# Second attention of a two-layer transformer kernel: queries computed with tokens over partitions, turned by DMA, and its side stages and first units placed anew

## The chip, the cores and the metric

The kernel runs on one core of one Trainium2 chip, in one launch. The metric is the device time of that launch in microseconds, as a median over runs.

## The reference, cut to what matters

2048 tokens (32 batches of 64) of width 512 pass four blocks, each added to x after a layer norm: a first cross attention, a feed-forward with 4-bit weights, a second cross attention, and a small routed memory with a gate. The change lies in the second attention:

```python
q = (layernorm(x) @ q_proj_w.T).reshape(B, Q, 32, 128)      # 32 query heads, 8 key heads
k = (ctx @ k_proj_w.T)...;  v = (ctx @ v_proj_w.T)...
q = w_q * q * rsqrt(mean(q * q, -1) + eps)                  # rmsnorm over the head's 128
k = w_k * k * rsqrt(mean(k * k, -1) + eps)
attn = softmax(q @ k.T / sqrt(128) + attention_mask)
x = x + (attn @ v) @ o_proj_w.T
```

The first attention has rotary positions in place of the norms.

## The kernel before, in words

**Units.** Both attentions are cut into 32 units: a group g of 8 (4 query heads, one key head) times a chunk c of 4 (512 tokens, 8 batches). `UNITS` lists them in order. Between the attentions lies the feed-forward, 24 steps of (s, c). Every product is made of halves: each operand is held as a 16-bit high part and a 16-bit low part, and three matmuls (`THREE`) replace one.

**Five engines, five programs.** `sync`, `tensor`, `scalar`, `vector` and `gpsimd` are written out by hand in program order and joined by semaphores (`signal`s). A wait holds up all that is behind it on that engine. SP (`sync`) has the only queue of DMAs: it issues the loads of weights, and the DMA transposes.

**A unit on TensorE** (`units`, L1160): `scores(u)`, then `front(u + 1)`, which is keys and values of unit u+1 (`keys_values`, L801) and four query tiles (`queries`, L817); then four tiles of the output product of unit u-1 (`output`, L865), and `weigh(u)` (L907), probabilities times values. In the second attention, `norm_q(u + 1)` (L886) stands between output tiles 2 and 3. PSUM has eight banks: the queries lie in 0, 1, 6, 7; keys and values in 2, 3; the scores in 4, 5; output tiles 0 to 3 in 2, 3, 0, 2; weighing in 0, 1, 6, 7. `bank(i, ...)` waits until what lay in the bank has been read.

**Queries of the second attention.** A head's query product has the head's 128 dimensions over partitions and 512 tokens along the row, the layout that scores needs. The norm is a sum over partitions, so ScalarE writes a high half (L1449), the squares (L1452) and the squares' high half (L1453); VectorE writes the query's low half (L2023); GpSimd writes the squares' low half (L2750); and TensorE sums the squares over partitions with 32 matmuls against a column of ones (L886). VectorE scales these sums (L2031), GpSimd raises them to the power -1/2 (L2758), and the softmax multiplies the scores by the result (L2082), then adds the mask (L2088).

**Keys of the second attention** have tokens over partitions. ScalarE sums their squares (L1423), VectorE multiplies by both norm weights (L2008), GpSimd takes the power (L2741) and scales (L2744). From unit 2 on ScalarE and GpSimd make the halves (L1430, L2735) and a DMA transpose turns them (L637); in units 0 and 1 TensorE turns them (`turn_k`, L874).

**Probabilities** are normalised on GpSimd (L2722), halved (L1470, L2729), and turned by DMA (L630), or by TensorE (L851, with L1477 and L2118 behind it) in units 0 and 31.

**Side stages.** `SIDE` is a table of other work, put by `plan(L, u, slot, stage)` at slots 0 to 9 of a unit: 0 after keys and values, 1 to 4 behind the query tiles, 5 to 8 behind the output tiles, 9 behind weighing. It holds the preparation of the next weights ("amax" L1330, "peak" L923, "scale" L1366, "low" L1933), layer norms ("ln_norm" L1499, "ln_turn" L936 and L1511, "ln_low" L1952), and the last block's stages. Weights of groups 0 and 1 of the second attention have their low halves made by GpSimd (L2686).

## Time and profile before

| | |
|---|---|
| median of 3 runs | 2425.37 us (2425.29 to 2427.68) |
| the profiled execution's own time | 2425.11 us |
| its span | 2423.3 us |
| granted TensorE clock, mean | 0.994 of 2.4 GHz |
| matmuls (PE) / weight loads | 2367.6 us, 98% / 1295.6 us, 53% |
| VectorE (DVE) / ScalarE (ACT) / GpSimd (POOL) | 67% / 52% / 51% |

The span is what the profiler records from the first to the last instruction; the time is some 2 us longer. PE stands for TensorE's matmuls, PEld for its weight loads, SPq for the queue of DMAs. "L886" is line 886 of the kernel. A row of the timeline merges neighbouring instructions of one line: start, duration, engine, line, operation, output<-inputs, shapes, count, and in brackets the idle time before with what ended it. A matmul's modelled end lies past its successor's start, so its cost on the path is the distance between starts.

### The profile page before, as it was taken

To read this page: it belongs to the slowest core of one execution; us is meant where nothing else is said; L and a number is where in the kernel's file an instruction comes from. 1 tells how busy PE (TensorE), PEld (TensorE's weight loads), DVE (VectorE), ACT (ScalarE), POOL (GpSimd) and SP (SyncE) were. 2 spreads that over 40 slices of the span, in tenths; PEclk is the share of its full clock that TensorE was granted. 3 is DMA by queue.
4 is the path that set the end of the run, shared out by engine and by line. 5 is a ranking of instruction groups with operands and counts; after the bars stand their busy time and mean duration, and the time that the engine had idled before them with its cause. 6 is when DMAs were issued, how large, how long until landed. Compare 5 with 4: busy or idle time off the path is not lost.

```text
span 2423.3 us, 45113 instructions
## 1 busy us (share of the span) xinstructions
PE 2367.6 (98%) x17668; PEld 1295.6 (53%) x17668; DVE 1625.1 (67%) x3133; ACT 1254.1 (52%) x2423; POOL 1227.8 (51%) x983
## 2 busy tenths in 40 slices
PE   8899999999999999999999999999999999999998
PEld 4455555555555555444444655555555555555554
DVE  7977777777777798754444666667666666656566
ACT  7666555656555545433232554555555555544443
POOL 4656566666666666233232445445555555445531
PEclk9999999999999999999999999999999999999999
DMA  6111121212121111011101011122121212221101
GB/s 211 45 45 36 44 53 27 53 27 53 32 53 31 42 40 28 27 44 36 44 11 29 27 31 28 44 53 62 36 62 36 62 36 62 53 43 27 27 14 70
DMA packets 216753, 108.13 MB, mean 45 GB/s; under 512 B 169280, under 2 KB 192480, under 8 KB 216544
## 3 DMA queue, kind: packets, MB, share of 16 engines
q1 hardware_dynamic: 216544, 105.25, 17.5%
q8 instruction: 142, 2.33, 0.4%
q14 instruction: 67, 0.55, 0.1%
HBM read 61.62 MB, written 4.19 MB: 27 GB/s over the span
## 4 chain that ended last, share of the span: by engine, by line
PE 65%; POOL 13%; DVE 11%; issue 5%; ACT 5%; DMA 0%; POOLq 0%; DVEq 0%; SPq 0%; ACTq 0%
PE PB L865 18%; PE PB L817 16%; PE PB L977 9%; PE PB L801 6%; PE PB L994 5%; POOL AR L2711 5%; POOL AR L2716 3%; POOL PSP L2729 2%; PE PB L907 2%; PE PB L842 2%; DVE AR L2128 2%; DVE WB L1933 2%; PE PB L773 2%; POOL AR L2706 1%; ACT JUNK L1330 1%
## 5 line engine op out<-in xcount | busy, mean ns | idle before, releaser
L865 PE MATMUL PB<-WB,AR 128*128 128x512 f16 x3072 | 685.5, 380 | 3.4 <-DVE XTB L1952 1.6
L817 PE MATMUL PB<-XTB,WB 128*128 128x512 f16 x3072 | 679.5, 380 | 1.2 <-DVE XTB L1952 0.7
L865 PEld LDWEIGHTS PB<-WB,AR 128*128 128x128 f16 x3072 | 298.3, 98 | 359.0 <-issue 11.1
L817 PEld LDWEIGHTS PB<-XTB,WB 128*128 128x128 f16 x3072 | 297.5, 98 | 345.3 <-issue 5.6
L2722 POOL TENSOR_TENSOR AR<-AR,SML 128x512 f32<-128x512 f32 x128 | 144.6, 1150 | 318.1 <-DVE SML L2113 318.1
L2143 DVE SCALAR_TENSOR_TENSOR X<-PB,SML,X 128x512 f32<-128x512 f32 x256 | 189.5, 747 | 169.4 <-PE PB L865 163.4
L1490 ACT ACTIVATE AR<-PB 128x512 f16<-128x512 f32 x256 | 132.0, 602 | 248.2 <-PE PB L907 248.2
L2023 DVE TENSOR_TENSOR AR<-PB,AR 128x512 f16<-128x512 f32 x128 | 88.2, 690 | 167.9 <-ACT AR L1453 167.9
L2711 POOL TENSOR_TENSOR AR<-AR,CST 128x512 f32<-128x512 f32 x128 | 183.0, 1430 | 33.9 <-ACT AR L1400 33.9
L977 PE MATMUL PB<-XTB,AR 128*128 128x512 f16 (+1 forms) x864 | 192.5, 379 | 0.0
L1994 DVE TENSOR_TENSOR AR<-AR 128x512 f16<-128x512 f32 x128 | 132.9, 1038 | 74.7 <-ACT AR L1406 74.5
L2716 POOL TENSOR_TENSOR AR<-AR 128x512 f32<-128x512 f32 x128 | 174.6, 1364 | 12.1 <-DVE AR L1985 2.3
L801 PE MATMUL PB<-WB,CTB 128*128 128x256 f16 x1536 | 173.1, 273 | 1.1 <-DVE WB L1933 0.9
L2128 DVE TENSOR_TENSOR AR<-PB,AR 128x512 f16<-128x512 f32 x256 | 158.6, 682 | 11.7 <-ACT AR L1490 11.7
L1985 DVE TENSOR_TENSOR AR<-PB,CST 128x512 f32<-128x512 f32 x128 | 88.2, 689 | 112.8 <-ACT AR L1400 112.8
L2758 POOL TENSOR_TENSOR SML<-SML 128x16 f32<-128x16 f32 (+1 forms) x33 | 98.4, 2982 | 128.9 <-DVE SML L2031 128.9
L1406 ACT ACTIVATE AR<-AR 128x512 f16<-128x512 f32 x128 | 80.5, 630 | 158.8 <-POOL AR L2716 157.4
L801 PEld LDWEIGHTS PB<-WB,CTB 128*128 128x128 f16 x1536 | 148.0, 98 | 18.7 <-issue 1.0
L2750 POOL TENSOR_TENSOR AR<-AR 128x512 bf16<-128x512 f32 x128 | 147.8, 1163 | 16.3 <-ACT AR L1453 16.3
L2702 POOL TENSOR_TENSOR AR<-AR,CST 128x512 f32<-128x512 f32 x32 | 44.6, 1394 | 216.7 <-ACT AR L1379 216.7
L2729 POOL TENSOR_TENSOR PSP<-AR,PSP 128x512 f16<-128x512 f32 x120 | 149.9, 1259 | 0.0
L2777 POOL TENSOR_TENSOR AR<-AR 128x512 f16<-128x512 f32 (+1 forms) x44 | 50.9, 1156 | 180.2 <-ACT AR L1574 180.2
(273 smaller groups left out, 3776.9 us busy)
## 6 DMA issues: line engine op xcount, KB each, us to landing
STG<-in_wo SPq DMA_DIRECT2D x14, 1024.0 KB
STG<-in_wq SPq DMA_DIRECT2D x13, 1024.0 KB
STG<-in_qw_gu SPq DMA_DIRECT2D x40, 128.0 KB
STG<-in_ctxT SPq DMA_DIRECT2D x4, 1024.0 KB
X<-in_x SPq DMA_DIRECT2D x4, 1024.0 KB, 10.3
out_x<-X SPq DMA_DIRECT2D x16, 256.0 KB, 2.4
STG<-in_wk SPq DMA_DIRECT2D x14, 256.0 KB
STG<-in_wv SPq DMA_DIRECT2D x14, 256.0 KB
```

Of the source, the lines that this page charges most:

```text
L801: m = pe.do.matmul(b[:, t2 * 256:(t2 + 1) * 256], CT[x][c][:, k, tok], wkv[y][:, k, :], start=n == 0, stop=n == 11)
L817: m = pe.do.matmul(b[:, :], wq[x][:, k, h * 128:(h + 1) * 128], XT[y][c][:, k, :], start=n == 0, stop=n == 11)
L865: m = pe.do.matmul(b[:, :], AT[x][:, h, t * 128:(t + 1) * 128], wo[y][:, h, :], start=n == 0, stop=n == 11)
L977: m = pe.do.matmul(b[0:wd, :], GUW[pl][x][:, k, cols], XT[y][c][:, k, :], start=e == 0, stop=e == 11)
L1994: dve.do.tensor_tensor(head_of(QT[1], h), by_batch(M1[h]), head_of(QT[0], h), ALU.subtract).then_inc(q_lo.of((0, u, h)), 1)
L2128: dve.do.tensor_tensor(lo, b[:, :].rearrange("p (b h q) -> p b h q", b=2, h=4), hi, ALU.subtract).then_inc(at_lo.of((L, u, j, odd)), 1)
L2143: dve.do.scalar_tensor_tensor(xs, PB[WB_OUT[t]][:, :], co(L, u, 0), xs, ALU.mult, ALU.add).then_inc(x_add.of((L, u, t)), 1)
L2711: pool.do.tensor_tensor(rt, rt, SINT.unsqueeze(1).to_broadcast([128, BC, SQ]), ALU.mult).then_inc(q_sin.of((u, h)), 1)
L2716: pool.do.tensor_tensor(M1[h], M1[h], RT[h], ALU.add).then_inc(q_add.of((u, h)), 1)
L2722: pool.do.tensor_tensor(v, v, RCT[:, cols].unsqueeze(2).to_broadcast([128, BC, SQ]), ALU.mult).then_inc(p_n.of((L, u, pair)), 1)
L2729: pool.do.tensor_tensor(PL[:, pair, :], SS[:, pair, :], PH[:, pair, :], ALU.subtract).then_inc(pl.of((L, u, pair)), 1)
L2750: pool.do.tensor_tensor(head_of(SQL, h), by_batch(M1[h]), head_of(SQH, h), ALU.subtract).then_inc(sql.of((u, h)), 1)
```

## The change

In the second attention:

- A query product is now one token tile of 128 by the group's four heads (512 columns): `XT` is stationary, the weights move. Two batches share a token tile, and `XT` of that norm is written with the tokens in the order query, then parity of the batch.
- ScalarE squares each head out of PSUM with a sum along the row (16 instructions of 128 columns), scales the four sums; GpSimd takes the power of 4 columns for each tile; ScalarE writes the scaled high halves (16 of 128 columns), VectorE the scaled low halves (16). SP turns them with three DMA transposes (2048, 1024 and 1024 columns). Scores read them with a step of two columns.
- The keys' scaling goes into their halves (4 instructions on ScalarE, 4 on VectorE); the product on GpSimd goes, and all units' keys are turned by DMA. `norm_q` and `turn_k` are gone from TensorE, `L2082` from the softmax, `L2744`, `L2735` and `L2750` from GpSimd.
- Layer norms and tail set-up use other banks and slots; weights' halves made by GpSimd in unit 1 move to slots 5 to 7.
- First units: keys and values of unit 1 and its first query tile precede unit 0's scores; unit 2's keys and values stand around unit 0's weighing; unit 0's probabilities are turned after query tile 2. In the first attention, the prologue's order and the slots of a layer norm and of chunk 2's preparation change.

```diff
+        QHP = [words(a, 1024, F16) for a in (10752, 5632)]
+        QHL = [QHP[t // 2][:, 1024 * (t % 2):1024 * (t % 2) + 1024] for t in range(4)]
+        QT_tiles = words(0, 2048, F16).rearrange("p (a n) -> p a n", n=128)
+        QT_rows = words(0, 2048, F16).rearrange("p (t a m o) -> p t a m o", t=4, a=4, o=2)
+        def rows_of(L, n, pair, b):
+            if L == 0:
+                return QT[n][:, (pair * BC + b) * 128:(pair * BC + b + 1) * 128]
+            return QT_rows[:, b // 2, 2 * n + pair, :, b % 2]
...
+            for half, (norm, turn, low) in enumerate(((0, 3, 3), (4, 6, 6)) if L == 0 else ((0, 2, 2), (3, 5, 6))):
...
-        plan(1, 1, 0, "scale", w(1, 1, 2))
+        plan(1, 1, 5, "scale", w(1, 1, 2))
-            plan(1, 1, 1 + half, "low", w(1, 1, 2), half)
+            plan(1, 1, 6 + half, "low", w(1, 1, 2), half)
-        plan_ln(1, 2, 2, 2)
-        plan_ln(1, 4, 2, 3)
+        for u, c in ((2, 2), (4, 3)):
+            plan(1, u - 1, 9, "ln_stats", 2, c)
+            for slot, *stage in ((4, "ln_norm", 0), (6, "ln_turn", 0), (6, "ln_low", 0), (6, "ln_norm", 1), (8, "ln_turn", 1),
+                                 (8, "ln_low", 1)):
+                plan(1, u, slot, stage[0], 2, c, *stage[1:])
...
+            def turn_q(u, part):                                   # SP
+                first, last = ((0, 2), (2, 3), (3, 4))[part]
+                for t in range(first, last):
+                    sp.wait_ge(q_hi, (1, u, t))
+                    sp.wait_ge(q_lo, (1, u, t))
+                if u > 0:
+                    sp.wait_ge(s_mm, (1, u - 1, 1))
+                else:
+                    sp.wait_ge(y_mm, (4, NC - 1, 3))
+                sp.do.dma_start_transpose(out=QT_tiles[:, 8 * first:8 * last, :],
+                                          in_=QHP[0] if part == 0 else QHL[first]).then_inc(qt_in.of((u, part), 16), 16)
...
+                    elif u < NU - 1:
+                        if by_dma(1, u):
+                            turn_p_pair(1, u, 0)
+                        turn_k(u + 1)
+                        if by_dma(1, u):
+                            turn_p_pair(1, u, 1)
+                        for part in range(3):
+                            turn_q(u + 1, part)
...
+            def queries_1(u, t):                                   # TensorE
+                b = bank(QB[t], (q_hi, (1, u, t)), (q_lo, (1, u, t)))
...
+                for k in range(KT):
+                    for x, y in THREE:
+                        m = pe.do.matmul(b[:, :], XT[x][c][:, k, t * 128:(t + 1) * 128], wq[y][:, k, :],
+                                         start=n == 0, stop=n == 11)
...
-            def turn_k(u):
-            def norm_q(u):
...
                 for u in range(NU - 1):                            # TensorE, units
                     scores(L, u)
                     front(L, u + 1, u)
...
+                    if (L, u) == (1, 0):
+                        keys_values(2, 0)
                     weigh(L, u)
                     side(L, u, 9)
+                    if (L, u) == (1, 0):
+                        keys_values(2, 1)
...
+            def squares_1(u, t):                                   # ScalarE
+                for h in range(4):
+                    n = 4 * t + h
+                    act.do.activation(M1[t][:, 128 * h:128 * h + 128], PB[QB[t]][:, 128 * h:128 * h + 128], ACTF.Square,
+                                      accum_out=RSQ[:, n:n + 1]).then_inc(q_sq.of((u, t)), 1)
+                act.wait_ge(q_sq, (u, t))
+                rs = RSQ[:, 4 * t:4 * t + 4]
+                act.do.activation(rs, rs, ACTF.Identity, scale=1.0 / DH, bias=eco(1, g, 0)).then_inc(q_ms.of((u, t)), 1)
+            def queries_1(u, t):
+                act.wait_ge(q_pow, (u, t))
...
+                for h in range(4):
+                    n = 4 * t + h
+                    act.do.activation(QHL[t][:, 128 * h:128 * h + 128], PB[QB[t]][:, 128 * h:128 * h + 128], copy,
+                                      scale=RSQ[:, n:n + 1]).then_inc(q_hi.of((1, u, t)), 1)
...
+                    for t in range(4):                             # ScalarE, front
+                        if (u, t) != (1, 0):
+                            squares_1(u, t)
+                        if t == 0 and by_dma(1, beside):
+                            halved_p(1, beside)
+                        if t == 1:
+                            halved_k(u)
+                        if t > 0:
+                            queries_1(u, t - 1)
+                        if (beside, t) == (0, 2):
+                            turned_p(1, 0)
+                        if t == 3:
+                            queries_1(u, 3)
+                        side(1, beside, 1 + t)
...
+            def low_1(u, t):                                       # VectorE
+                dve.wait_ge(q_pow, (u, t))
+                dve.wait_ge(q_hi, (1, u, t))
+                for h in range(4):
+                    n, cols = 4 * t + h, slice(128 * h, 128 * h + 128)
+                    dve.do.scalar_tensor_tensor(QHL[t][:, 512 + 128 * h:640 + 128 * h], PB[QB[t]][:, cols], RSQ[:, n:n + 1],
+                                                QHL[t][:, cols], ALU.mult, ALU.subtract).then_inc(q_lo.of((1, u, t)), 1)
...
+                    halved_k(u)                                    # VectorE, front
+                    for t in range(4):
+                        side(1, beside, 1 + t)
+                        low_1(u, t)
...
-                    for h in range(4):                             # GpSimd, front
-                        queries_1(u, h)
+                    for t in range(4):
+                        power_1(u, t)
+                        if t < 2 and by_dma(1, beside):
+                            halved_p(1, beside, t)
```

## Rows read from the trace of the kernel before

**Rows 1.** The page's first part: busy us, share of the span, instructions.

```profile
PE 2367.6 (98%) x17668; PEld 1295.6 (53%) x17668; DVE 1625.1 (67%) x3133; ACT 1254.1 (52%) x2423; POOL 1227.8 (51%) x983
```

**Rows 2.** Table of stretches: length; PE, PEld, DVE, ACT, POOL busy; clock; DMA share, GB/s.

```profile
1420.00:2340.00 920.00, 910.04 (x7543) 529.88 (x7541) 585.06 (x1215) 474.27 (x1084) 465.18 (x378) 0.99 0.20 44
```

**Rows 3.** TensorE's timeline of one typical unit of the second attention.

```profile
1908.00 2.75 PE L817 MATMUL PB<-XTB,WB 128*128 128x512 f16 x12
1910.59 7.93 PE L865 MATMUL PB<-WB,AR 128*128 128x512 f16 x36
1918.36 0.94 PE L886 MATMUL PB<-ONEB,AR 128*128 128x1 bf16 x32
1919.17 2.75 PE L865 MATMUL PB<-WB,AR 128*128 128x512 f16 x12
1921.85 1.48 PE L907 MATMUL PB<-AR 64*128 64x256 f16 x24
1923.27 1.57 PE L842 MATMUL PB<-AR 128*128 128x64 f16 x48
```

**Rows 4.** TensorE's timeline of the second attention's unit 0.

```profile
1382.96 0.60 PE L874 MATMUL PB<-CST,AR 128*128 128x128 f32 x4
1383.39 2.78 PE L801 MATMUL PB<-WB,CTB 128*128 128x256 f16 x24
...
1401.77 0.63 PE L874 MATMUL PB<-CST,AR 128*128 128x128 f32 x4 [1.55 <-ACT AR L1477]
...
1403.27 2.74 PE L907 MATMUL PB<-AR 64*128 64x256 f16 x24
```

**Rows 5.** TensorE in unit 1, and its waits at L886: total, times, longest.

```profile
1435.91 4.90 PE L865 MATMUL PB<-WB,AR 128*128 128x512 f16 x12
...
PE PB L886 <- POOL AR L2750: 4.6, 3, 4.0
```

**Rows 6.** TensorE's timeline of the first attention's start.

```profile
49.36 0.86 PE L842 MATMUL PB<-AR 128*128 128x64 f16 x24 [3.40 <-DVE AR L1994]
50.69 4.44 PE L817 MATMUL PB<-XTB,WB 128*128 128x512 f16 x12 [0.47 <-DVE WB L1933]
...
68.81 2.74 PE L907 MATMUL PB<-AR 64*128 64x256 f16 x24 [4.06 <-DVE AR L2118]
```

**Rows 7.** Weight loads by form: count, busy us, mean ns, idle before.

```profile
L886 PEld LDWEIGHTS PB<-ONEB,AR 128*128 128x128 bf16 x1024 | 30.1, 96 | 12.5 <-issue 6.2
L936 PEld LDWEIGHTS PB<-CST,LNB 128*128 128x128 f32 x192 | 21.4, 140 | 13.3 <-issue 8.2 <-DVE XTB L1952 2.2 <-DVE AR L2011 0.6
...
L923 PEld LDWEIGHTS PB<-IDB,SML 128*128 128x128 bf16 x55 | 5.4, 98 | 12.6 <-issue 4.3 <-DVE SML L1882 2.4 <-ACT JUNK L1330 0.4
```

**Rows 8.** ScalarE's timeline in the unit of rows 3.

```profile
1902.43 0.27 ACT L1423 ACTIVATE AR<-PB 128x128 f32<-128x128 f32 x1
1902.58 0.20 ACT L1423 ACTIVATION_READ_ACCUMULATOR AR<-PB 128x1 f32 x1
...
1907.01 1.17 ACT L1470 ACTIVATE PSP<-AR 128x512 f16<-128x512 f32 x2
...
1912.24 1.71 ACT L1366 ACTIVATE WB<-STG,SML 128x256 f16<-128x256 f32 x4
```

**Rows 9.** VectorE and GpSimd by form, 1700 to 2280 us: busy us, mean ns.

```profile
L2023 DVE TENSOR_TENSOR AR<-PB,AR 128x512 f16<-128x512 f32 x75 | 51.8, 691 | 95.4 <-ACT AR L1453 95.4
...
L2750 POOL TENSOR_TENSOR AR<-AR 128x512 bf16<-128x512 f32 x76 | 87.2, 1157 | 2.9 <-ACT AR L1453 2.9
...
L2741 POOL TENSOR_TENSOR SML<-SML 128x4 f32<-128x4 f32 x18 | 18.3, 1016 | 0.0
```

**Rows 10.** SP's transposes (ns min/median/max; landing), and a stretch that holds three.

```profile
L630 SPq DMA_TRANSPOSE AR<-PSP x120: 1232/1233/1442, 96.0 to 2324.3; - x120
...
DMA to landing us min/median/max: 3.0/3.1/5.0
...
1911.20:1917.00 5.80, 5.80 (x28) 2.65 (x27) 2.89 (x8) 2.75 (x7) 4.54 (x5) 1.00 0.69 130
```

More of the change, by code:

```diff
@@ L378, in plan_ln @@
                 plan(L, u - 1, 9, "ln_stats", i, c)
-            for half, (norm, turn, low) in enumerate(((0, 2, 2), (3, 5, 6))):
+            for half, (norm, turn, low) in enumerate(((0, 3, 3), (4, 6, 6)) if L == 0 else ((0, 2, 2), (3, 5, 6))):
                 plan(L, u, norm, "ln_norm", i, c, half)
@@ L529, in ln_banks @@
                 return 2, 3
-            return (4, 5) if (i, c) in IN_FFN else ((2, 3), (1, 6))[half]
+            if i == 2 and c > 1:
+                return (4, 3) if half else (4, 5)
+            return 4, 5
         def unpack_banks(s, k):
@@ L868, in output @@
                 m.then_inc(wo_mm.of((L, u, t)), 1)
-            def turn_k(u):
-                b = bank(4, (kt_hi, (1, u)), (kt_lo, (1, u)))
-                pe.wait_ge(k_mul, u)
-                for t in range(4):
-                    m = pe.do.transpose(b[:, t * 128:(t + 1) * 128], KF[:, t * 128:(t + 1) * 128], IDN)
-                m.then_inc(kt_mm.of(u), 1)
-            def norm_q(u):
-                bk = bank(5, (q_ms, u))
-                pe.wait_ge(q_sq, (u, 3))
-                pe.wait_ge(sql, (u, 3))
-                pe.wait_ge(ones_ok, "ones")
-                for pair in range(2):
-                    for b in range(BC):
-                        o = bk[:, pair * BC + b:pair * BC + b + 1]
-                        for n, s in enumerate((SQH, SQL)):
-                            m = pe.do.matmul(o, rows_of(s, pair, b), ONEB[:, 0:1], start=n == 0, stop=n == 1)
-                m.then_inc(qn_mm.of(u), 1)
             def weigh(L, u):
@@ L1281, in tensor @@
             keep_warm(8, 0)
[L1282 to L1283 removed]
+            queries_0(0, 0)
+            queries_0(0, 1)
+            queries_0(0, 2)
+            queries_0(0, 3)
             peak(w(0, 1, 0), 5)
[L1285 to L1286 removed]
             keys(1)
@@ L1303, in tensor @@
             keys_values(0, 0)
+            down(*FFN[-1])
             keys_values(0, 1)
-            down(*FFN[-1])
+            for t in range(4):
+                queries_1(0, t)
             ln_turn(2, 1, 1)
-            for h in range(4):
-                queries(1, 0, h)
             keys_values(1, 0)
-            turn_k(0)
             keys_values(1, 1)
-            norm_q(0)
+            queries_1(1, 0)
             units(1)
@@ L1856, in scalar @@
                 side("f", s, c, 3)
+            act.do.activation(TBL, CST[:, 0:1], ACTF.Exp).then_inc(t_act.of("table"), 1)
             values_1(0, 0)
             values_1(0, 1)
+            for t in range(4):
+                squares_1(0, t)
+                if t == 1:
+                    halved_k(0)
+                if t > 0:
+                    queries_1(0, t - 1)
+            queries_1(0, 3)
             ln_turn(2, 1, 1)
-            for h in range(4):
-                queries_1(0, h)
-            keys_1(0)
-            act.do.activation(TBL, CST[:, 0:1], ACTF.Exp).then_inc(t_act.of("table"), 1)
+            values_1(1, 0)
+            values_1(1, 1)
+            squares_1(1, 0)
             units(1)
@@ L2656, in vector @@
             values_1(0, 0)
+            down(*FFN[-1])
             values_1(0, 1)
-            down(*FFN[-1])
+            halved_k(0)
+            for t in range(4):
+                low_1(0, t)
             ln_low(2, 1, 1)
-            for h in range(4):
-                queries_1(0, h)
-            keys_1(0)
-            norm_q(0)
+            unit_scale(1, 1)
+            values_1(1, 0)
+            values_1(1, 1)
             units(1)
@@ L2840, in units @@
                     for slot in range(5, 9):
-                        if L and slot == 7:
-                            norm_q(u + 1)
                         side(L, u, slot)
@@ L2896, in gpsimd @@
             keys_1(0)
-            for h in range(4):
-                queries_1(0, h)
-            norm_q(0)
+            for t in range(4):
+                power_1(0, t)
             units(1)
```

347 lines of the change are left out of this document (151 added, 196 removed).

## The prediction

> **What bounds the kernel now.** I read the page's first part: TensorE's matmuls are busy 98% of the span, the next engine, VectorE, 67% [rows 1]. Busy time of pipelined matmuls proves little by itself, so the table of stretches came next: from 1420 to 2340 us, where the second attention's units 1 to 30 lie, TensorE has work for 910.0 of 920.0 us at a granted clock of 0.99 [rows 2]. So in a typical unit nothing waits on purpose: what TensorE no longer executes comes off the time, and what another engine does costs nothing until TensorE waits for it. The timeline of one unit [rows 3] gives the prices. Then the waits of TensorE show where it does stand still: the first units of both attentions [rows 4 to 6].
>
> **What goes from TensorE.** The sums of squares of the queries (L886, 32 matmuls of one column) start at 1918.36, and the next product starts at 1919.17 [rows 3]: 0.81 us of TensorE time. The group has 1024 matmuls, so 32 units [rows 7]: **-25.9 us**. The two key transposes by TensorE go too (L874, 8 matmuls in all); the first four took 1382.96 to 1383.39, 0.43 us [rows 4], so **-0.9**.
>
> In unit 1 the sums waited 4.0 us for GpSimd's square halves (L2750), and behind that pause the clock fell: the next 12 products took 4.90 us where 2.75 is usual [rows 5, 3]. The halves are gone, and GpSimd's weight halves move to slots 6 and 7, where TensorE needs nothing of them in that unit: 4.0 + 2.15 = **-6.2**. The two other waits of that kind made 0.6 us: **-0.6**. In unit 0, the wait at L874 (1.55) and 2.74 instead of 1.48 us for the weighing behind it [rows 4, 3] come to **-2.8**.
>
> **What comes to TensorE.** Query products: 12 of 512 columns for each of four tiles, before and after; only the operands trade places. L865 already has tokens as the stationary operand and costs the same for twelve as L817, 2.75 us [rows 3]: **0**. Scores: the same 48 matmuls, but their stationary operand is now every second column (token order is query, then batch parity). No row has that view. Below, 0: L923 loads a step-0 view in 98 ns, like the dense load of L886 in 96. Above, 42 ns for each of 48 x 32 = 1536 loads, if a 2-byte element with step 2 loads like a 4-byte one, 140 ns at L936 [rows 7]: +64.5 us. I take 0, since the nearer row is the one of the same element type, and keep the other end.
>
> The Trainium skill (SBUF — State Buffer, Specifications (TRN2)) says that consecutive accesses should hit a 16-byte line at least twice, which step-2 halves do; by it the price is 0 too.
>
> **The new chain behind the queries, and what covers it.** Times are those of the unit of rows 3. The last query tile's product ends at 1910.6. Then come: ScalarE's four squares with sums and a small scaling, GpSimd's power, ScalarE's four scaled copies, VectorE's four lows, the transpose, then scores. Prices [rows 8, 9]:
> - A square of 128 columns out of PSUM: 0.27 us alone; its accumulator read starts 0.15 later. Issued back to back I take 0.25 each, four and the scaling 1.4. If nothing overlaps it is 0.27 + 0.20 = 0.47 each.
> - A scaled copy of 128 columns: four of 256 columns took 1.71 us (L1366), four of 128 I take at 1.0.
> - GpSimd's power of 4 columns: 1.01 us (L2741).
> - A low of 128 columns: L2023 has 0.69 for 512; a quarter is 0.17, a start on top 0.28; four 1.1 (0.7 to 2.8).
> - A transpose: 1.23 us of SP's time, 3.0 to 3.1 to landing [rows 10].
>
> So ScalarE needs 2.4 us for each query tile, which takes TensorE 2.6 (1908.00 to 1910.59): it keeps pace. But values, exponent and a weight's squares come first; I put its start at 0.6 us behind the first tile, with the exponent 1.4 us earlier than now, since the softmax loses one pass over each pair (L2082, of L2023's size, 2 x 0.69). From there to the last tile's squares it has three tiles' squares (4.3), the probability halves (L1470, 1.17), the key halves (1.0) and two tiles' copies (2.0), 8.5 us, while TensorE makes three tiles in 7.8: a lag of 1.3. So squares 1911.9 to 1913.3, last copies 1915.3, VectorE's last low 1916.6. Two deadlines follow:
> - VectorE adds output tile 0 after the last low, by 1917.4. Output tile 3 reuses that bank; without the sums it starts at 1918.4. Margin **1.0 us**.
> - The last transpose lands at 1919.7; scores start at 1923.27 - 0.81 = 1922.5. Margin **2.8 us**.
>
> Hence a typical unit waits for nothing: **0**. SP: a unit has seven 1024-column transposes' worth instead of three, 7 x 1.23 = 8.6 us in a unit of about 920 / 30 = 30.7. The three cost the DMA engines 0.69 x 5.8 = 4.0 us, seven 9.3 [rows 10]. Behind them on SP queue the next weight load, whose area comes free only at slot 8, behind output tile 3, and the next unit's probabilities: both later than 1919. GpSimd loses 4 x 1.16 and more and gains 4 x 1.02 [rows 9]: it is no bound. VectorE loses 6 x 0.69 and gains 20 lows of 0.28, 5.6: +1.5 us in a unit in which it has rest.
>
> Two edits lie under other work: ScalarE's table load now stands before the first values, while TensorE has keys, values and a down product to run, and the last down product gets banks of its own: **0**.
>
> **New first units.** Unit 0's probabilities are turned by TensorE after two query tiles behind the scores (1.4 + 5.2 = 6.6 us) instead of four. Its softmax needs six passes of 0.69 and then exponent, sum, reciprocal and GpSimd's product, some 3 us for the first pair and 1 to 1.5 more for the second, 8.1 to 8.6: a wait of 1.9. Scores of unit 1 wait for their transpose, a chain of 1.2 + 1.0 + 1.0 + 1.1 + 3.1 = 7.4 us behind 6.7 of cover: 0.7. With a clock dip like that of rows 4 (1.3): **+3.9**. Layer norms (units 2, 4) and the last units (27 to 30) give ScalarE further activations where it is tight; I allow 0.8 us in each of six, **+5** (0 to 10).
>
> **The first attention.** Its start has TensorE waits of 3.40 and 4.06 us, with slow products behind each (4.44 for 2.75, 2.74 for 1.48) [rows 6]. ScalarE now turns two query heads before a weight's squares, VectorE spreads its layer-norm sums and mask, and the norm's turns move a slot later into other banks. Between nothing and the 10.4 us of the two; I take **-4**.
>
> **Sum**, against the profiled execution's own 2425.1 us (span 2423.3; the median of the runs shown is 2425.4): -25.9 - 0.9 - 6.2 - 0.6 - 2.8 - 4 + 3.9 + 5 = -31.5, so **2393.6 us**, given as 2394.
>
> **Rivals.**
> - *B, ScalarE and VectorE set the unit.* If squares don't overlap, 0.2 us on each of 16 takes 3.2 us per unit and the margin of 1.0 at output tile 3 is gone, 2.2 us over. For it: the two rows of L1423, 0.47 us together. Against: the read starts 0.12 us before the square ends [rows 8], and the new squares don't wait for each other. Halfway, 1 us of wait in each of 30 units: +30, **2424**; with the whole 2.2, 2460.
> - *A, the strided weight load.* This is the one that ends slower: every scores matmul waits for its load. Now a pair takes 1.41 us / 48 = 29 ns, and a load-bound one at L886 0.81 / 32 = 25 ns. Twice that is 51, +21 ns x 1536 = 33 us, 2427; at the 42 ns of rows 7 +64.5, 2458. Middle **2443**. It ends slower once a load costs over 20 ns more (31.5 us / 1536). For it: no row shows step 2. Against: the step-0 load.
> - *C, only the products' time comes off* and first units wait as before: -26.8, **2398**, inside the forecast's range.
>
> The Trainium skill (TensorE: Matmul & The Clock Gate, Weight-path perf modes) says weights are read 32 bits at a time, two bf16: by that, half of each read is lost with step 2, which is A; the same table allows a strided pattern.
>
> **How the numbers follow.** Forecast (with C) 0.70, 2382 to 2408: the lower end takes 10 us in the first attention and no new waits, the upper doubles the new ones. B 0.18, 2408 to 2440. A 0.12, 2427 to 2458. A difference of 0.2% (4.9 us) is about the least that a measurement of this kernel tells from none. Faster: 0.70 + half of B = 0.79. Same: 0.06, slower 0.15, from the rest of B and A. The range 2382 to 2424 leaves out A and the far half of B, 0.21.
>
> **What would show it.** No L886 group; from the last query tile's end to the scores 11.9 us against 12.7; scores' 48 still 1.41 us (A: 2.4 or more); no wait before output tile 3 or before scores in typical units (B: VectorE's output adds or the lows named as releasers); ScalarE busy some 4 us more per unit; no 4 us pause in unit 1, and waits under 4 us in all in unit 0. The forecast is wrong if those 11.9 us are over 12.3, or if the second attention's total of waits exceeds the 10 us of now.

## The result, and the profile after

The kernel became slower. Median of 4 runs 2440.17 us (2438.87 to 2441.48) against 2425.33 of the kernel before beside it; ratio 1.006, 95% interval 1.0047 to 1.0072. The profiled execution has a span of 2439.1 us, against 2423.3.

First line of the page's first part, to be read beside [rows 1]:

```profile
PE 2355.2 (97%) x16628; PEld 1277.1 (52%) x16636; DVE 1688.3 (69%) x3547; ACT 1391.7 (57%) x3799; POOL 1043.9 (43%) x888
```

1032 weight loads fewer, the 1024 of L886 and the 8 of L874, as the diff says. TensorE's busy time falls by 12.4 us where those products alone were priced at 26.8: other matmuls got slower. The table of stretches, same columns as [rows 2]:

```profile
1420.00:2340.00 920.00, 892.26 (x6579) 509.79 (x6579) 645.50 (x1593) 606.51 (x2366) 296.52 (x290) 0.99 0.39 77
1361.00:1420.00 59.00, 50.77 (x358) 31.32 (x356) 34.24 (x91) 38.91 (x156) 14.37 (x15) 0.94 0.26 49
```

TensorE now has no work for 27.7 us of these 920, before for 10.0. So look first at the unit that should have none of it, TensorE's timeline beside [rows 3]:

```profile
1914.81 10.52 PE L920 MATMUL PB<-WB,AR 128*128 128x512 f16 x48
1925.26 1.48 PE L943 MATMUL PB<-AR 64*128 64x256 f16 x24
1926.68 1.57 PE L897 MATMUL PB<-AR 128*128 128x64 f16 x48
1928.09 5.41 PE L841 MATMUL PB<-WB,CTB 128*128 128x256 f16 x48
```

No pause. From the end of the query tiles to the scores 11.87 us (forecast 11.9), scores to the next product 1.41. From scores to scores 28.94 us against 29.74: the 0.80 that was priced. The loss is elsewhere. Starts of the scores (L842 before, L897 after), and a layer norm turn near the feed-forward's end (L936 at 1349.71, L972 at 1357.41), cut the span so. The forecast is cut the same way, from its own terms (0.81 for each sum of squares, 0.8 for each of the six units with further activations, the first units' terms in the second stretch):

| stretch | before | forecast | after |
|---|---|---|---|
| start to the feed-forward's end | 1349.7 | -4 | +7.7 |
| to the scores of unit 3 | 124.8 | -9.0 | +3.0 |
| units 3 to 23 | 627.2 | -16.2 | -10.9 |
| units 24 to 30 | 237.4 | -2.5 | +16.8 |
| from the scores of unit 31 | 84.2 | 0 | -0.9 |
| span | 2423.3 | -31.7 | +15.8 |

(The forecast's sum is -31.5: it rounds six times 0.8 to 5.)

The waits behind the largest losses, all from TensorE's timeline (start, duration, and in brackets the pause before with what ended it):

```profile
123.99 1.97 PE L972 MATMUL PB<-CST,LNB 128*128 128x128 f32 x8 [3.69 <-DVE SML L1942]
...
974.88 0.26 PE L985 MATMUL PB<-WB 4*128 4x256 f16 x1 [3.37 <-DVE XTB L2008]
...
975.21 4.06 PE L920 MATMUL PB<-WB,AR 128*128 128x512 f16 x12
...
1413.30 1.39 PE L943 MATMUL PB<-AR 64*128 64x256 f16 x12 [2.48 <-ACT AR L1499]
1416.48 1.47 PE L943 MATMUL PB<-AR 64*128 64x256 f16 x12 [1.80 <-DVE AR L2085]
1421.03 0.29 PE L959 MATMUL PB<-IDB,SML 128*128 128x128 bf16 x1 [3.08 <-ACT JUNK L1366]
1421.13 5.31 PE L841 MATMUL PB<-WB,CTB 128*128 128x256 f16 x24
...
1662.22 2.76 PE L920 MATMUL PB<-WB,AR 128*128 128x512 f16 x12 [1.49 <-DVE X L2191]
...
2155.54 5.30 PE L920 MATMUL PB<-WB,AR 128*128 128x512 f16 x12 [4.75 <-ACT STG L1625]
...
2219.42 1.94 PE L1060 MATMUL PB<-CST,LNB 128*128 128x128 f32 x8 [4.40 <-DVE LNB L2341]
2221.15 3.37 PE L856 MATMUL PB<-WB,XTB 128*128 128x512 f16 x12
```

All but three are for a side stage. In the order of the rows: in the first attention, unit 2's layer norm turn waits for bank 4, which the maxima of a context chunk's preparation hold (L1942 reads them); unit 30's unpacking waits for banks 4 and 5, which the layer norm's turn holds (before, it had 2, 3, 1, 6); in unit 0 of the second attention a small product waits 3.08 us for ScalarE's squares of a weight; in unit 25 output tile 0 waits for bank 2, where a set-up product lies that ScalarE reads only after all its query work; in unit 27 (and 29, 4.33) the last part's turn waits for VectorE's normalization. The three others are the query chain itself: in unit 0 the attention product waits 2.48 us for ScalarE's scaled copies and 1.80 for VectorE's low halves, and in unit 8 output tile 3 waits 1.49 us for VectorE's addition of output tile 0 (L2191), which comes behind the last low halves. That is the wait for which the forecast had a margin of 1.0 us.

Behind the long ones the next products run at up to twice their usual time (12 products in 2.75, 24 in 2.8): the granted clock is 0.50 from 1421.13 to 1426.23 and from 2155.54 to 2160.77, that is at its lower level, 1.2 instead of 2.4 GHz. ScalarE and VectorE in unit 27 show why the normalization is late:

```profile
2215.43 1.26 ACT L1469 ACTIVATE AR<-AR,SML 128x128 f16<-128x128 f32 x4
...
2212.05 0.48 DVE L2068 TENSOR_SCALAR SML<-SML 128x4 f32<-128x4 f32 x1
2216.78 2.04 DVE L2077 SCALAR_TENSOR_TENSOR AR<-AR,SML 128x128 f16<-128x128 f32 x4 [4.25 <-issue]
2218.74 0.99 DVE L2341 TENSOR_SCALAR LNB<-X,SML 128x512 f32<-128x512 f32 x2
```

VectorE's low halves of the keys (L2077) come after a pause of 4.25 us. The row names no releaser, but they need ScalarE's high halves (L1469), which end 0.1 us ahead of them; and the normalization (L2341), which needs neither, stands behind them.

### The profile page after: what moved, and what is told of

It is laid out like the page before. It is cut to its first block and busy times, and to the rows that moved or that the text cites. A ratio compares the mean times of both kernels' runs of the same rounds, so it can differ in the third digit from the quotient of the medians.

```text
span 2439.1 us, 45180 instructions
## 1 busy us (share of the span) xinstructions
PE 2355.2 (97%) x16628; PEld 1277.1 (52%) x16636; DVE 1688.3 (69%) x3547; ACT 1391.7 (57%) x3799; POOL 1043.9 (43%) x888
## 5 line engine op out<-in xcount | busy, mean ns | idle before, releaser
L871 PE MATMUL PB<-XTB,WB 128*128 128x512 f16 x1536 | 343.2, 382 | 2.2 <-DVE WB L1986 1.0
L856 PE MATMUL PB<-WB,XTB 128*128 128x512 f16 x1536 | 341.5, 381 | 0.0
L2191 DVE SCALAR_TENSOR_TENSOR X<-PB,SML,X 128x512 f32<-128x512 f32 x256 | 187.4, 746 | 81.5 <-PE PB L920 74.9
L871 PEld LDWEIGHTS PB<-XTB,WB 128*128 128x128 f16 x1536 | 149.1, 99 | 176.4 <-issue 8.8
L856 PEld LDWEIGHTS PB<-WB,XTB 128*128 128x128 f16 x1536 | 150.0, 98 | 173.8 <-issue 4.4
L2761 POOL TENSOR_TENSOR AR<-AR,CST 128x512 f32<-128x512 f32 x128 | 181.9, 1421 | 31.3 <-ACT AR L1436 31.3
L2766 POOL TENSOR_TENSOR AR<-AR 128x512 f32<-128x512 f32 x128 | 173.3, 1354 | 11.7 <-DVE AR L2041 1.9
L2085 DVE SCALAR_TENSOR_TENSOR AR<-PB,SML,AR 128x128 f16<-128x128 f32 x512 | 143.6, 342 | 48.7 <-POOL SML L2793 45.8
L2077 DVE SCALAR_TENSOR_TENSOR AR<-AR,SML 128x128 f16<-128x128 f32 x128 | 60.8, 534 | 164.5 <-issue 148.9
L2793 POOL TENSOR_TENSOR SML<-SML 128x4 f32<-128x4 f32 x128 | 128.8, 1007 | 101.9 <-ACT SML L1487 101.9
L2176 DVE TENSOR_TENSOR AR<-PB,AR 128x512 f16<-128x512 f32 x256 | 158.6, 681 | 12.6 <-ACT AR L1537 12.6
```

What stands on the lines that cost most here:

```text
L856: m = pe.do.matmul(b[:, :], XT[x][c][:, k, t * 128:(t + 1) * 128], wq[y][:, k, :], start=n == 0, stop=n == 11)
L871: m = pe.do.matmul(b[:, :], wq[x][:, k, h * 128:(h + 1) * 128], XT[y][c][:, k, :], start=n == 0, stop=n == 11)
L2085: dve.do.scalar_tensor_tensor(QHL[t][:, 512 + 128 * h:640 + 128 * h], PB[QB[t]][:, cols], RSQ[:, n:n + 1], QHL[t][:, cols], ALU.mult, ALU. ...
L2176: dve.do.tensor_tensor(lo, b[:, :].rearrange("p (b h q) -> p b h q", b=2, h=4), hi, ALU.subtract).then_inc(at_lo.of((L, u, j, odd)), 1)
L2191: dve.do.scalar_tensor_tensor(xs, PB[WB_OUT[t]][:, :], co(L, u, 0), xs, ALU.mult, ALU.add).then_inc(x_add.of((L, u, t)), 1)
L2761: pool.do.tensor_tensor(rt, rt, SINT.unsqueeze(1).to_broadcast([128, BC, SQ]), ALU.mult).then_inc(q_sin.of((u, h)), 1)
```

## The experiments

Two theories. **S**: the query layout is as cheap as forecast, and what costs the time are side stages that the change put into other banks, slots and places in an engine's order. **L**: the layout itself costs it, ScalarE and VectorE being fuller; then mending one side stage only moves its wait. All edits are made in the changed kernel. Medians of 5 runs unless said, ratio to the kernel before on the same chip (its median was 2424.8 to 2425.6). The runs were made on several chips, so a difference in us between the medians of two edited kernels is good to about 1 us at best.

**The first attention put back**

```
-for half, (norm, turn, low) in enumerate(((0, 3, 3), (4, 6, 6)) if L == 0 else ((0, 2, 2), (3, 5, 6))):
+for half, (norm, turn, low) in enumerate(((0, 2, 2), (3, 5, 6))):
-plan_at(0, ("c", 2), (1, 9), (2, 2, 4), (2, 5), (2, 8), (2, 9))
+plan_at(0, ("c", 2), (1, 9), (2, 0, 6), (2, 1), (2, 7), (2, 9))
...
+if (i, c) in {(0, 2), (0, 3), (1, 0)}:
+    return (1, 6) if half else (2, 3)
...
+side(0, u, 5)
 queries_0(u + 1, 3)
-for slot in range(5, 10):
+for slot in range(6 if L == 0 else 5, 10):
```
and the order of the first products and of VectorE's and ScalarE's first work. The last four lines put ScalarE's side stage of slot 5 ahead of its last query head again, in every unit of the first attention.

> The changed kernel with the first attention put back as it was before: the order of its first products and VectorE operations, its layer norm stages' slots and banks, the preparation of the third context chunk. The second attention is untouched. In the trace of the changed kernel the query product that opens the second attention's work starts 7.7 us late (L972 at 1357.41 us, before at 1349.71). Theory S (the side stages' new banks and slots cost the time, the query layout itself is as cheap as forecast): the whole 7.7 us come back, 2440 to 2432 us, between 2430 and 2434, and the second attention's unit lengths stay. Theory L (the query layout costs it: fuller ScalarE and VectorE, 48 more transposing DMAs, and what comes early is waited for later): the time stays within 2 us of 2440.

(Its "48 more" DMAs is a slip: the transposes of keys and queries go from 30 to 128.)

Measured 2434.93 us, 1.0043 (1.0031 to 1.0056): 5.2 us back; the second attention starts 6.4 us earlier (1390.1 instead of 1396.5). Theory S in kind, a little less in size.

**Only its banks and slots put back**, with ScalarE's place for slot 5; the new starting order kept.

> Only the layer norm stages' slots and banks of the first attention (and the preparation of the third context chunk) put back, the new order of the first products and VectorE operations kept. With both put back the time fell by 5.2 us, and the scores of unit 1 started 0.9 us later than in the changed kernel. Theory S (the waits at unit 2, 3.69 us, and unit 30, 3.37 us, are for banks 4 and 5 now shared by the stages): nearly all of it is the banks', 2434 us or a little less, 2432 to 2436. Rival P (the new order at the start costs it): 2438 to 2441.

Measured 2434.70, 1.0041 (1.0028 to 1.0053). The banks and slots (with slot 5's place on ScalarE, which no run separates from them) are all of it. The new starting order is not shown to be worth anything. With it the scores lie 0.8 to 1.0 us earlier than in the run before from unit 1 on, but the seven kernels whose first attention is put back whole differ by 1.6 us among themselves where the feed-forward ends (1349.9 to 1351.5), and this one, at 1350.1, lies among them. I had taken 4 us. The four that keep the changed first attention lie at 1356.3 to 1358.8, so the loss itself is clear of that scatter.

**VectorE's side stage of slot 1 first**

```
-halved_k(u)
 for t in range(4):
     side(1, beside, 1 + t)
+    if t == 0:
+        halved_k(u)
     low_1(u, t)
```

> One line moved in the changed kernel: in the second attention VectorE does the side stage of slot 1 ahead of the keys' low halves instead of behind them. Only units 27 and 29 have such a stage (the last part's normalization, whose product waits 4.40 and 4.33 us there, both followed by a stretch at the lower clock; these two units are 40.05 and 41.23 us long, before 35.07 and 34.99). Theory S: both waits fall under 1 us, the units come back to about 34 to 35 us, and the time is 10 us less, 2430 us, between 2427 and 2433. Theory L: ScalarE's work on the queries is what these units wait for in the end, the wait moves to the next product behind it, and less than 2 us is gained, 2438 to 2441.

Measured 2431.84, 1.0032 (1.002 to 1.0045): 8.3 us back. Units 27 and 29 fall from 40.05 and 41.23 to 36.43 and 36.36 us. What is left stands one stage later, in this kernel's timeline of TensorE:

```profile
2215.51 1.04 PE L1060 MATMUL PB<-CST,LNB 128*128 128x128 f32 x8
...
2227.04 1.09 PE L1060 MATMUL PB<-CST,LNB 128*128 128x128 f32 x8 [2.72 <-DVE LNB L2341]
```

The first turn no longer waits; the second now does.

**The set-up products of unit 25 later**

```
-plan(1, 25, 4, "tail_setup", 0); plan(1, 25, 5, "tail_setup", 1)
+plan(1, 25, 6, "tail_setup", 0); plan(1, 25, 8, "tail_setup", 1)
```
with banks 4, 5, 1 and 5, 4 for 2, 3, 4 and 5, 1.

> The five small products that set up the last part move from slots 4 and 5 of unit 25 to slots 6 and 8, and from banks 2, 3, 4, 5, 1 to 4, 5, 1, 5, 4, where ScalarE reads them at once and no output tile waits for the bank. In the changed kernel output tile 0 of unit 25 waits 4.75 us for ScalarE's copy of bank 2, and its 12 products then take 5.30 us at the lower clock. Theory S: the wait goes with its clock loss, unit 25 falls from 39.7 to about 35 us, the time by 3 to 5 us, to 2436 (2434.5 to 2437.5). Theory L: the unit is bound by ScalarE's work, and the time stays within 1.5 us of 2440.

Measured 2433.95, 1.004 (1.0027 to 1.0052): 6.2 us back, more than either theory had. Unit 25 falls from 39.67 to 32.15 us, where I had expected about 35; it lies well under the 36.13 of the kernel before too. There the same set-up products made two short waits (0.41 and 0.84 us) with 24 products in 7.04 us behind them, where 5.34 is usual.

**The maxima's small product one unit later**

```
-plan(1, 0, 9, "peak", w(1, 1, 2), 4)
+plan(1, 1, 3, "peak", w(1, 1, 2), 4)
```

> The small product that turns the row of maxima of the second head group's output weights moves from slot 9 of unit 0 to slot 3 of unit 1 of the second attention. In the changed kernel it waits 3.08 us for ScalarE's squares there, and the scores behind it run at 1.95 us for 48 instead of 1.41 and the product after that at 5.31 for 24. Theory S: 3 us of wait and about 2 us of clock come back, 2435.5 us (2434 to 2437.5). Theory L: what follows waits for the unit's queries all the same, and the time stays within 1.5 us of 2440.

Measured 2437.37, 1.0052 (1.0038 to 1.0065): 2.8 us back. In the trace the scores of unit 1 start 4.6 us earlier against a common start, of which 2.1 is lost again in the next: output tile 3 of unit 1 waits 3.29 us there instead of 1.96.

**All four together**

> The four edits of the first four runs together in the changed kernel: the first attention as before, VectorE's side stage of slot 1 ahead of the keys' low halves, the five small set-up products of unit 25 later and in other banks, the maxima's small product one unit later. Alone they took 5.2, 8.3, 6.2 and 2.8 us off 2440.17. Theory S (four separate waits of side stages, the query layout cheap): they add up, 2440.2 - 22.5 = 2417.7 us, between 2413 and 2421, under the kernel before by 4 to 12 us, which is what the layout gives. Theory L (each edit only gives slack back that one shared limit, the work on the queries, takes again): the sum falls short by a third or more, over 2425.

Measured 2415.45, ratio 0.9961 (0.9947 to 0.9975), and -24.7 us where the four alone make -22.5. They add up. A shared limit behind these four waits is ruled out, and with it Theory L as the account of the loss. What is left of it are the waits for the query chain in units 0, 1 and 8: unit 8 takes 30.8 to 30.9 us in every kernel without extra copies.

The combined kernel is faster than the one before, by 10 us on the same chip. Not all of this is the query layout: unit 25 lies 4.0 us under the kernel before, where the layout gives 0.8. The later set-up products could be had in the kernel before as well, which was not tried.

**How much room ScalarE has.** The combined kernel with extra 128x512 copies ahead of the squares of query tile 3, two or six per unit.

> The combined kernel with extra copies of 128x512 constants on ScalarE (taken as 0.6 us each) ahead of the squares of query tile 3: two of them beside units 7 to 13, six beside units 14 to 20 of the second attention. It measures the margin that the prediction gave the new work: 1.0 us ahead of output tile 3 (whose bank VectorE frees after the last low halves), 2.8 us ahead of the scores. If the margins are right: 0.2 us more per unit in the first seven (up to 1.5 us in all), about 2.6 us more per unit in the second seven (some 18 us in all, less if the wait at the output tile is made up). If ScalarE's work on the queries already sets the unit (Theory L): 1.2 us more per unit and 3.6 us more per unit, 34 us in all.

Measured (2 runs) 2451.26. The total, 35.8 us over the combined kernel, is close to what I had written for Theory L, so the total does not decide; the units do. With two copies units 9 to 13 take 29.3 to 29.4 us (+0.4, not 1.2); only unit 8, which waits for the chain already, takes 2.9 more. With six, five of the seven units take 33.6 to 33.7 us (+4.7) and units 15 and 19 take 31.95 (+3.0). Timeline of TensorE in one unit with two copies (11) and two with six (18 and 19), and ScalarE's six copies:

```profile
1745.68 2.76 PE L923 MATMUL PB<-WB,AR 128*128 128x512 f16 x12 [0.26 <-DVE X L2203]
...
1969.28 4.21 PE L923 MATMUL PB<-WB,AR 128*128 128x512 f16 x12 [2.90 <-DVE X L2203]
...
2002.86 2.76 PE L923 MATMUL PB<-WB,AR 128*128 128x512 f16 x12 [2.90 <-DVE X L2203]
...
1959.40 3.95 ACT L1490 ACTIVATE JUNK<-IDB 128x512 bf16<-128x512 bf16 x6
```

A copy takes 3.95 / 6 = 0.66 us. Two are 1.32 and leave a wait of 0.26 at output tile 3; six are 3.95 and leave 2.90. Both give the same room: 1.05 us, at the product and with the releaser that the forecast named, for 1.0 forecast. What I had wrong here is the price of a wait. The same 2.90 us are followed by 12 products in 4.21 us in unit 18 (granted clock 0.64) and in 2.76 in unit 19 (1.00). So a wait of 2.9 costs 3.0, or 4.7 where the clock falls, which it did in five units of seven.

**Two more edits for the last part**

```
-... (u, 4, ("t_norm", c, 1)), ... (u + 1, 4, ("t_lg", c)), ...
+... (u, 3, ("t_norm", c, 1)), ... (u + 1, 6, ("t_lg", c)), ...
-TB_R, TB_A, TB_LG, TB_W = (2, 2, 7), (3, 3, 1), (4, 4, 4, 1), (1, 2, 4)
+TB_R, TB_A, TB_LG, TB_W = (4, 4, 7), (5, 5, 1), (4, 4, 4, 1), (1, 2, 4)
```

> The combined kernel with two more edits to the last part's stages in units 27 to 30: the second half of the normalization at slot 3 instead of 4 (with the earlier edit alone the product of slot 6 waits 2.72 us for it), and the two products of slot 3 of units 28 and 30 in banks 4 and 5 instead of 2 and 3, the small one of slot 4 at slot 6 (output tile 0 waits 1.52 us in each of these units for VectorE's read of bank 2 or 3). Theory S: both waits go, about 2 x (2.7 + 1.5) = 8 us less what the neighbours take, 3 to 9 us under the combined kernel. Theory L: no more than 1 us under it.

Measured 2415.62, 0.9963 (0.995 to 0.9975): nothing over the combined kernel. Units 28 and 30 fell as expected, from 36.01 and 36.45 to 34.33 and 34.76, but 27 and 29 rose from 36.46 and 36.39 to 40.24 and 38.78. Of the 3.8 us more in unit 27, 2.4 are the slow clock: the 24 products behind the wait take 7.73 us instead of 5.34. The wait itself stayed (2.74 us). A miss, and VectorE's timeline of this kernel says why:

```profile
2202.98 1.13 DVE L2088 SCALAR_TENSOR_TENSOR AR<-PB,SML,AR 128x128 f16<-128x128 f32 x4 [1.24 <-POOL SML L2796]
2207.64 1.85 DVE L2344 TENSOR_SCALAR LNB<-X,SML 128x512 f32<-128x512 f32 x2 [3.53 <-POOL X L2828]
2209.41 2.15 DVE L2088 SCALAR_TENSOR_TENSOR AR<-PB,SML,AR 128x128 f16<-128x128 f32 x8
```

The second half waits 3.53 us for GpSimd (L2828 adds the first half to X out of the same buffer), and the low halves of query tile 2 now wait behind it. In the combined kernel GpSimd does that sum only here:

```profile
2207.18 1.01 POOL L2796 TENSOR_TENSOR SML<-SML 128x4 f32<-128x4 f32 x1 [2.36 <-ACT SML L1489]
2208.16 2.48 POOL L2828 TENSOR_TENSOR X<-X,LNB 128x512 f32<-128x512 f32 x2
```

behind its fourth power (L2796), with 2.36 us of rest in front of it, for the change had put all four powers ahead of GpSimd's side stages.

**GpSimd's side stages of slots 1 and 2 behind the third power**, on top of the kernel before this.

```
 for t in range(4):
     power_1(u, t)
     if t < 2 and by_dma(1, beside):
         halved_p(1, beside, t)
-for t in range(4):
-    side(1, beside, 1 + t)
+    for slot in ((), (), (1, 2), (3, 4))[t]:
+        side(1, beside, slot)
```

> The kernel with the last part's two edits (second half of the normalization at slot 3, the two products of units 28 and 30 in banks 4 and 5), and GpSimd's side stages of slots 1 and 2 behind its third power instead of behind its fourth. There the wait for the normalization stayed (2.74 and 2.67 us in units 27 and 29), and in the combined kernel VectorE's second half starts 0.16 us after GpSimd's sum that reads the first half's buffer, which stands behind all four powers (sum at 2208.16 us, though VectorE had written the buffer by 2198.9). Theory G (GpSimd's order keeps the buffer): units 27 and 29 fall from 36.5 and 36.4 us in the combined kernel to about 34.5, units 28 and 30 to 34.3 and 34.8, in all 7 us less than the combined kernel's 2415.5: 2408.5, between 2406 and 2411. Rival V (VectorE's and ScalarE's own work on the queries is the wait): as the kernel without the GpSimd edit, 2414 to 2417.

Measured 2406.76, 0.9927 (0.9914 to 0.9941). Units 27 to 30 take 34.38, 34.33, 34.31 and 34.75 us, as forecast. Theory G holds here: GpSimd's order is what made the earlier slot pay. TensorE in unit 27, where 0.69 is left in place of the 2.74, now for ScalarE's scaled copies:

```profile
2206.52 0.60 PE L1062 MATMUL PB<-CST,LNB 128*128 128x128 f32 x4
2207.80 0.63 PE L1062 MATMUL PB<-CST,LNB 128*128 128x128 f32 x4 [0.69 <-ACT AR L1501]
```

**GpSimd's order alone**, on the combined kernel.

> The combined kernel with GpSimd's order alone changed (side stages of slots 1 and 2 behind its third power), the normalization's second half still at slot 4 and the banks 2 and 3 kept. Theory G: VectorE comes to slot 4 only behind the low halves of query tile 2 (they end at 2209.4 us in the combined kernel, 0.2 us ahead of the normalization), so the buffer is free earlier for nothing: within 1 us of the combined kernel's 2415.5. Rival: the GpSimd order is all there is, 4 us or more less.

Measured 2413.07 (4 runs), 0.9953 (0.9939 to 0.9966). The combined kernel had 0.9961 (0.9947 to 0.9975): the intervals overlap, so the 2.4 us between the two medians are not shown to be a gain. The waits say more than the totals. In units 27 and 29 the wait for the normalization is 1.62 and 1.55 us instead of 2.75 and 2.67, and each unit is 1.1 us shorter (35.33, 35.26). That is more than Theory G allowed the order alone, and less than its rival had. Units 28 and 30 are longer by 1.7 and 1.6 (37.69, 38.02), but not by the edit. TensorE in unit 28, in the combined kernel and in this one:

```profile
2245.69 10.53 PE L922 MATMUL PB<-WB,AR 128*128 128x512 f16 x48 [1.54 <-DVE CTB L2368]
...
2241.03 12.22 PE L922 MATMUL PB<-WB,AR 128*128 128x512 f16 x48 [1.52 <-DVE CTB L2368]
```

The same products wait the same time in both; behind it the granted clock is 1.00 in one trace and 0.86 in the other. Units 0 to 2 are the same case the other way round (86.4 us against 88.5). In unit 2 the wait is 1.8 us in both, and the 24 products behind it take 5.34 us here and 6.87 there, 1.5 of the 2.1 us; the kernel with the last part's two edits and the old order has 86.5. So two traces of the same code can differ by up to 1.7 us at each such place, and a unit's length says little without its waits.

**Both halves of unit 2's keys ahead of unit 0's attention product**

```
 if (L, u) == (1, 0):
     keys_values(2, 0)
+    keys_values(2, 1)
 weigh(L, u)
 side(L, u, 9)
-if (L, u) == (1, 0):
-    keys_values(2, 1)
```

> The kernel of the run before in this series, and in unit 0 of the second attention both halves of unit 2's keys and values ahead of unit 0's attention product, where the second half stands behind it now. In the combined kernel that product waits 2.49 us for ScalarE's copy of a query tile and 2.36 us for VectorE's low halves, and the 24 products behind it take 4.28 us at the lower clock instead of 2.8. Theory S: the 2.6 us of keys and values cover the first wait and part of the clock's loss, 2.5 to 5 us less than the same kernel without it. Rival (what follows, the scores of unit 1, waits for the transposed queries in their place, which come about 3 us after the last low halves): less than 1 us.

Measured 2405.49, 0.9922 (0.9909 to 0.9934): 1.3 us under the same kernel without it (2405.0 to 2406.1 against 2405.9 to 2407.1, so the runs nearly touch). The first wait is gone, and the rival's took its place, with slow scores behind it. TensorE in unit 0:

```profile
1406.18 0.83 PE L945 MATMUL PB<-AR 64*128 64x256 f16 x12
1409.29 0.83 PE L945 MATMUL PB<-AR 64*128 64x256 f16 x12 [2.29 <-DVE AR L2087]
1412.72 2.72 PE L899 MATMUL PB<-AR 128*128 128x64 f16 x48 [2.60 <-DMA AR<-AR]
```

Both theories miss: the gain is under the 2.5 us of S, since the rival's wait came, and over the rival's 1. This is the best version: 19.3 us (0.8%) under the kernel before, 34.7 under the changed one.

## Why the prediction was wrong

The first line of this last kernel's page, against [rows 1]:

```profile
PE 2340.9 (97%) x16628; PEld 1271.9 (53%) x16636; DVE 1686.7 (70%) x3547; ACT 1393.3 (58%) x3799; POOL 1046.9 (44%) x888
```

2367.6 - 2340.9 = 26.7 us of TensorE's work fewer, for the 25.9 + 0.9 of the forecast. That it agrees to a tenth is partly luck, since both totals hold stretches at the slow clock (mean 0.994 and 0.993). The typical unit shows the same price without them, 28.94 us for 29.74. That step was right, and it was the change. The forecast failed in the untypical units: side stages whose place and banks I had priced at nothing or at 0.8 us, and the new first units. The steps in turn:

- **Products removed, -26.8: right.** 0.80 us per typical unit. The changed kernel's TensorE executes the same 16628 matmuls in 14.3 us more than the best version's, which fits the slow clock behind its waits (mean 0.986).
- **The chain behind the queries, 0: right in a typical unit, with its margin.** Forecast 1.0 us at output tile 3, measured 1.05. In unit 8 the margin is used up: ScalarE's exponent there waits 2.92 us for VectorE (1.02 in unit 9), the chain comes later, and output tile 3 waits 1.49. The prices held singly as well. ScalarE in the changed kernel, 1700 to 2280 us (busy us, mean ns), and its timeline:

```profile
L1499 ACT ACTIVATE AR<-PB,SML 128x128 f16<-128x128 f32 x304 | 85.3, 360 | 1.7
L1483 ACT ACTIVATE AR<-PB 128x128 f32<-128x128 f32 x304 | 79.7, 284 | 11.1 <-PE PB L856 10.5
L1483 ACT ACTIVATION_READ_ACCUMULATOR AR<-PB 128x1 f32 x304 | 66.2, 218 | 0.0
...
1914.69 1.12 ACT L1499 ACTIVATE AR<-PB,SML 128x128 f16<-128x128 f32 x4
1915.68 0.29 ACT L1483 ACTIVATE AR<-PB 128x128 f32<-128x128 f32 x1
1915.84 0.23 ACT L1483 ACTIVATION_READ_ACCUMULATOR AR<-PB 128x1 f32 x1
1915.93 0.30 ACT L1483 ACTIVATE AR<-PB 128x128 f32<-128x128 f32 x1
```

  Four copies 1.12 (1.0 forecast); square and read of its sum overlap, one pair 0.25 us behind the other, so rival B's condition did not arise. The low halves: four in 1.12 (1.1).
- **The strided load, 0: right.** By form, 1500 to 2100 us, against [rows 7]:

```profile
L897 PEld LDWEIGHTS PB<-AR 128*128 128x128 f16 x960 | 29.1, 98 | 4.2 <-issue 4.2
```

  98 ns, as with step 0 and as dense. Rival A, which was to end slower, was not what happened; that the time fell in its range (2427 to 2458) is chance. The rule of the Trainium skill (TensorE: Matmul & The Clock Gate, Weight-path perf modes) that weights are read 32 bits at a time, two bf16, gave no price here. With the one that accesses should hit a 16-byte line at least twice (SBUF — State Buffer, Specifications (TRN2)), as they do at this step, the row agrees.
- **The first attention, -4: wrong by 11.7 us.** I priced the new starting order and wrote of the norm's turns "a slot later into other banks" without asking who else holds those banks. Banks 4 and 5 at unit 2 hold a preparation's maxima, at unit 30 the layer norm and the unpacking share them; 6.4 us of the 7.7 went with the first attention put back. Of the 4 us that I took for the new starting order, no run shows any. I never laid out the banks of one unit side by side.
- **New first units, wrong by 12 us.** The pause of unit 1 went, as forecast, though output tile 3 behind it now waits 1.96 us (2.28 in the best version, with its 12 products in 4.45). Its place was taken in unit 0, with waits of 2.48, 1.80 and 3.08 us and two under 1, 8.5 in all, where I had 1.9 + 0.7. The query tiles of unit 1 no longer have keys and values ahead of them, so ScalarE has no head start. And the small product of the maxima ("peak"), at slot 9 of unit 0 as before, now needs squares that ScalarE comes to only behind its whole query work; I did not look at it: 2.8 us.
- **Units 3 to 23, -16.2: 5.3 short.** Three units hold nearly all of it. Unit 4 is 2.2 us over its forecast (34.54 for 32.3). Its layer norm's turn waits 1.77 us, and the 24 products behind it take 7.03 us; with the first attention put back and the second untouched the same wait is 1.76, and they take 5.34. So 1.7 of it is the clock:

```profile
1538.25 1.33 PE L972 MATMUL PB<-CST,LNB 128*128 128x128 f32 x8 [1.77 <-ACT LNB L1546]
1539.42 7.03 PE L920 MATMUL PB<-WB,AR 128*128 128x512 f16 x24
...
1534.08 1.33 PE L974 MATMUL PB<-CST,LNB 128*128 128x128 f32 x8 [1.76 <-ACT LNB L1548]
1535.24 5.34 PE L922 MATMUL PB<-WB,AR 128*128 128x512 f16 x24
```

  Unit 8 is 1.7 over (30.84, the wait of 1.49 above), and unit 23 is 1.3 over (30.27: a small product waits 1.04 for ScalarE's squares of a weight).
- **Last units, +5 for all layer norms and units 27 to 30: wrong by 19 us,** the largest error. I took 0.8 us in each of six units for further activations. The stages' durations were indeed covered; what I left out is their place in an engine's order. Three places in the code said it: VectorE's side stages behind `halved_k`, which waits for another engine; GpSimd's behind four powers; and the set-up products, which ScalarE reads 4.4 us later in unit 25 than it did. In none of them did the stage itself get longer; each stands behind a wait, in front of something that another engine waits for. Mended, this stretch is under the forecast.
- **The clock.** I gave the two waits that were to go a clock price, and the new first units one dip of 1.3 us; the rest had none. Unit 27 with 4.40 us of wait is 5.7 us longer than in the best version, and 2.90 us of wait made 3.0 or 4.7.

Of the signs that the forecast named against itself, the first did not come (11.87 us, under 12.3) and the second did: TensorE without work for 27.7 us, over the 10 of before.

Even the best version, with its mended side stages and edits that the forecast kernel did not have, does not reach the sum. By the same stretches:

| stretch | forecast | after | best version |
|---|---|---|---|
| start to the feed-forward's end | -4 | +7.7 | +0.4 |
| to the scores of unit 3 | -9.0 | +3.0 | +2.2 |
| units 3 to 23 | -16.2 | -10.9 | -12.5 |
| units 24 to 30 | -2.5 | +16.8 | -8.3 |
| from the scores of unit 31 | 0 | -0.9 | -1.9 |
| span | -31.7 | +15.8 | -20.1 |

Open, and not tried: the layer norms of units 2 and 4 of the second attention (34.53 and 32.85 us in the best version where a typical unit takes 28.9), the first units' remaining waits, unit 8, and the better places of side stages in the kernel before.

## What to carry to other kernels

A forecast for a typical unit can be right to a tenth of a microsecond while the few untypical units decide the sign. After pricing the main chain, list for each side stage what stands ahead of it on its engine and who else uses its bank, before and after: a wait for another engine that moves in front of a stage costs as much as a longer stage. And give a pause of TensorE, here from 1.5 us on, a possible surcharge for the slow clock behind it, here mostly 1.5 to 1.7 us. Whether it comes differs between two traces of the same code, so compare waits before unit lengths.

## What the runs showed of the hardware

- The same pause of TensorE is sometimes followed by the lower clock and sometimes not. With six extra copies the pause ahead of output tile 3 is 2.84 to 2.90 us in seven units; the 12 products behind it take 4.21 to 4.45 us in five of them and 2.76 in two.
- Shorter pauses do it too: behind 1.52 to 1.54 us in unit 28, 48 products take 10.53 us in the combined kernel and 12.22 in the one with GpSimd's order alone; behind 1.76 and 1.77 in unit 4, 24 products take 5.34 or 7.03. In both pairs the products ahead of the pause in the unit are the same, so neither they nor its length alone tells whether the clock falls.
- A stationary operand with a step of two 2-byte elements loads in 98 ns, as a dense one.
- Four scaled copies of 128 columns out of PSUM on ScalarE took 1.12 us, and a square of 128 columns with the read of its sum follows the one before by 0.25 us, though the two rows alone are 0.28 and 0.22.
